# A graph network kernel: three node tiles fetched by TensorE in two turns of three, and the work between its two layers in another order

## What is computed

```python
h = jnp.maximum(_layernorm(x, axis=-1), 0.0)
x = x + layer_one(h, node_vec1, src, dst, edge_attr_4, edge_attr_64, ...)
h = jnp.maximum(_layernorm(x, axis=-1), 0.0)
# layer two, per edge and then per node:
ss, vv = (s[src], v[src])
out0 = C0 * (ss * e0 @ W1 + dot * INV3 @ W2)
out1 = C1 * (p3 + p4 + p5)          # products of ss, vv with e0, e1
m_agg = jax.ops.segment_sum(m, dst, num_segments=n)
x = x + jax.nn.relu(m_agg through Ws, Wv) + h
```

## Time and profile before

| | us |
|---|---|
| median of 3 runs | 1985.27 (1984.33 to 1985.97) |
| the profiled execution, its time | 1984.93 |
| its span, first to last instruction | 1983.0 |
| GpSimd busy | 1434.7 (72%) |
| TensorE busy | 1687.1 (85%) |
| VectorE busy | 1275.5 (64%) |
| ScalarE busy | 174.6 (9%) |

### The profile page before, as it was taken

One profiled execution on the slowest core, in us unless ns is written; L12 is line 12 of the kernel. 1 busy time (PEld: TensorE's weight loads), 2 busy tenths in 40 slices (PEclk: granted clock), 3 DMA queues, 4 the chain that ended last, 5 costly groups with the idle time before them and its releaser, 6 DMA issues.

```text
span 1983.0 us, 52527 instructions
## 1 busy us (share of the span) xinstructions
PE 1687.1 (85%) x15596; PEld 1447.7 (73%) x15596; DVE 1275.5 (64%) x2725; ACT 174.6 (9%) x392; POOL 1434.7 (72%) x1531
## 2 busy tenths in 40 slices
PE   6988999889898888998867878888787878788787
PEld 4766676767676666676647878787787878788787
DVE  6887888788877787787866444454544445454543
ACT  5100000000000010001050000000000000000000
POOL 2777777777777777777736777777777777777774
PEclk9999999999999998999978999898989989898988
DMA  6333333333333333333313232223232332332323
GB/s 234 104 101 102 102 103 101 103 102 102 102 103 101 103 102 102 102 103 101 102 41 87 70 75 72 73 72 73 72 74 70 74 74 70 74 74 70 74 71 83
DMA packets 112032, 179.50 MB, mean 91 GB/s; under 512 B 30382, under 2 KB 79212, under 8 KB 111628
## 3 DMA queue, kind: packets, MB, share of 16 engines
q0 software_dynamic: 71904, 122.81, 25.3%
q1 hardware_dynamic: 35208, 51.38, 8.2%
q10 hardware_dynamic: 4644, 2.19, 0.4%
HBM read 170.11 MB, written 6.14 MB: 89 GB/s over the span
## 4 chain that ended last, share of the span: by engine, by line
POOL 64%; issue 22%; PE 8%; DVE 2%; DMA 2%; ACT 1%; POOLq 1%; DVEq 0%; ACTq 0%
POOL g L663 64%; PE w_ps L953 2%; PE sums L942 2%; DMA g<-node_table,src 1%; PE sums L963 1%; PE sums L953 1%; PE w_ps L469 1%; DVE work L814 1%; PE w_ps L905 1%; PE sums L938 0%; ACT H L281 0%; POOLq L657 0%; DVE work L808 0%; PE hid_ps L891 0%; PE w_ps L1115 0%
## 5 line engine op out<-in xcount | busy, mean ns | idle before, releaser
L663 POOL DMA_INDIRECT g<-node_table,src x1498 | 1420.2, 948 | 487.0 <-issue 472.9
L942 PE MATMUL sums<-g,sel 128*128 128x160 f32 x1612 | 292.2, 343 | 158.4 <-DMA g<-node_table,src 157.3
L953 PE MATMUL w_ps<-H,work 128*128 128x160 f32 x2900 | 405.2, 300 | 2.6 <-DVE work L778 2.6
L953 PEld LDWEIGHTS w_ps<-H,work 128*128 128x128 f32 x2900 | 398.0, 191 | 2.9 <-DVE work L778 2.9
L942 PEld LDWEIGHTS sums<-g,sel 128*128 128x128 f32 x1612 | 269.7, 222 | 171.3 <-DMA g<-node_table,src 139.0
L814 DVE TENSOR_TENSOR work<-w_ps,g 128x384 f32<-128x384 f32 (+3 forms) x693 | 298.7, 459 | 107.1 <-DMA g<-node_table,src 56.6
L833 DVE STREAM_TRANSPOSE turned<-sums 128x160 f32<-128x160 f32 x232 | 80.0, 345 | 433.4 <-PE sums L963 296.7
L905 PE MATMUL w_ps<-fc_sb,work 64*128 64x224 f32 x1612 | 239.4, 397 | 88.4 <-DVE work L808 76.3
L938 PEld LDWEIGHTS sums<-work,sel 128*32 128x32 f32 x6448 | 201.6, 113 | 110.6 <-issue 72.9
L905 PEld LDWEIGHTS w_ps<-fc_sb,work 64*128 64x128 f32 x1612 | 174.0, 200 | 135.8 <-DVE work L808 106.4
L761 DVE TENSOR_TENSOR sel<-mixed,sh 128x896 f32<-128x896 f32 x232 | 251.7, 1085 | 27.7 <-DVE mixed L757 2.2
(11 more groups left out here) (81 smaller groups left out, 524.1 us busy)
## 6 DMA issues: line engine op xcount, KB each, us to landing
g<-node_table SPq DMA_DIRECT2D x2304, 0.6 KB
feat<-edge_feat_dram SPq DMA_DIRECT2D x60, 512.0 KB
g<-node_table,src POOLq DMA_INDIRECT x1498
g<-node_table ACTq DMA_DIRECT2D x1152, 0.6 KB
named<-src_rows_dram SPq DMA_DIRECT2D x30, 128.0 KB
X<-x_dram SPq DMA_DIRECT2D x5, 400.0 KB, 6.6
node_table<-H SPq DMA_DIRECT2D x5, 400.0 KB, 2.7
named<-src_rows_dram SPq DMA_DIRECT2D x30, 64.0 KB
```

The lines of the kernel that those rows point to most:

```text
L663: nc.gpsimd.indirect_dma_start(out=g[:, slot(p, u, j), :], out_offset=None, in_=table[layer], in_offset=bass.IndirectOffsetOnAxis(ap=src[: ...
L942: last = nc.tensor.matmul(sums[:, o % 2, 0:D], sel[:, o % 2, j, :], g[:, slot(p, o % UNROLL, j), :], **first_last)
L953: last = nc.tensor.matmul(found_at[:, i, 0:D], match[layer][:, i, t, :], H[:, t, :], start=(t == 0), stop=(t == NT - 1))
```

## The change

1. In layer two, in turns p = 0 and p = 1 of each period, TensorE fetches tile 6 of group 1 too (`MORE_AT`, `PICK_ROWS`): 18 fetches more and 18 gathers less. The third match has a buffer of its own, in `acc0`, which layer one no longer needs, and the numbers of the semaphores are computed anew (`pick_number`). Names for three picks instead of two are loaded every turn.
2. In the last turn of layer one (groups 112 to 115) the fetch for group 114 and its match are gone, and GpSimd gathers that tile.
3. Between the layers ScalarE computes all 25 gates first, then two square roots (parts of 18 and 7 tiles), then normalises tiles 0 to 10. VectorE normalises tiles 11 to 24, in two rounds of seven, as a scale and shift per tile and one maximum with zero over all seven. The table is written in four pieces (6, 5, 7 and 7 tiles), and VectorE adds `H` to `X` in two steps ahead of layer two's preparation.

```diff
-ROOTS = (0, 11, 21, NT)
+ROOTS = (0, 18, NT)
+BY_ACT = 11
+PIECES = (0, 6, BY_ACT, 18, NT)
...
+MORE_AT = ((), (0,1))
+PICK_ROWS = ((2,), (0, 1, 2))
...
-        acc0 = sb("acc0", [ROWS[0], 2, ACC_W])
+        acc0_all = sb("acc0", [P, 2, ACC_W])
+        acc0 = acc0_all[0:ROWS[0], :, :]
...
-        match = (acc1[:, 1:2, 0:NPAD].rearrange("p b (t e) -> p b t e", e=P),
-                 work[:, 0:2 * NPAD].rearrange("p (b t e) -> p b t e", b=2, e=P))
+        by_tile = lambda row: row.rearrange("p (t e) -> p t e", e=P)
+        match = ((by_tile(acc1[:, 1, 0:NPAD]),),
+                 (by_tile(work[:, 0:NPAD]), by_tile(work[:, NPAD:2 * NPAD]), by_tile(acc0_all[:, 0, 0:NPAD])))
...
-            picked = PICKED[layer]
-            picks = len(picked)
-            by_pool = [TILES - (u in picked) for u in range(UNROLL)]
-
-            def pick_after(o, s, ahead):
-
-
-                u = (o + ahead) % UNROLL
-                if not own_weights and u in picked and (s is None or s + ahead < GROUPS):
-                    return picked.index(u), (o + ahead) // UNROLL
+            more_at, pick_rows = MORE_AT[layer], PICK_ROWS[layer]
+
+            def picks_of(p):
+
+                return pick_rows if p in more_at else PICKED[layer]
+
+            def picks_before(f, p, e):
+
+                n = len(more_at)
+                return len(PICKED[layer]) * f + (n * e + (n if p < 0 else sum(m < p for m in more_at)) if n else 0)
+
+            def pick_number(f, p, e, i, nxt=0):
+
+                if nxt:
+                    f, p, e = f + 1, (p + 1 if p != PERIOD - 1 else 0), (e + 1 if p in (-1, PERIOD - 1) else e)
+                return picks_before(f, p, e) + i
+
+            def pick_after(o, s, p, ahead):
+
+                u, nxt = (o + ahead) % UNROLL, (o + ahead) // UNROLL
+                then = picks_of((p + 1) % PERIOD if nxt and p >= -1 else p)
+                if not own_weights and u in then and (s is None or s + ahead < GROUPS):
+                    return then.index(u), nxt
                 return None
+
+            def fetched(p, s, u):
+
+                return u in picks_of(p) and not (own_weights and s is not None and s >= GROUPS - UNROLL)
...
-                    tiles = min(tiles_of(UNROLL * it + u), by_pool[u] - by_row_at(p, u, TILES - 1))
+                    tiles = min(tiles_of(UNROLL * it + u), TILES - fetched(p, UNROLL * it + u, u) - by_row_at(p, u, TILES - 1))
...
-                        if o == 1 and (s is None or s < GROUPS):
-                            put(f, 0, 0, s == 1)
+                        if o == 1:
+                            if fetched(p, s, 2):
+                                put(f, p, e, 2, 0, 0, s == 1)
+                            else:
+                                act.sem_inc(found_copied, 1)
                     else:
                         if s == 0:
-                            put(f, 0, 0, True)
-                        if pick_after(o, s, 1):
-                            put(f, *pick_after(o, s, 1), s is not None and s + 1 < UNROLL)
+                            put(f, p, e, 0, 0, 0, True)
+                        if pick_after(o, s, p, 1):
+                            put(f, p, e, (o + 1) % UNROLL, *pick_after(o, s, p, 1), s is not None and s + 1 < UNROLL)
...
                     if not fresh:
-                        dve.wait_ge(found, picks * f + (picks * nxt + i + 1 - picks))
+                        dve.wait_ge(found, m if own_weights else m - 1)
                     wide = [P, NT, P]
-                    nc.vector.tensor_tensor(match[layer][:, i, :, :], wanted.unsqueeze(1).to_broadcast(wide),
+                    nc.vector.tensor_tensor(match[layer][i], wanted.unsqueeze(1).to_broadcast(wide),
...
-                                compare(f, 0, 1, False)
+                                if s == GROUPS - 1 - UNROLL:
+                                    dve.wait_ge(named_in[layer], 16 * f + 32)
+                                    dve.sem_inc(named_read, 1)
+                                    dve.sem_inc(match_done, 1)
+                                else:
+                                    compare(f, p, e, 2, 0, 1, False)
...
-                            find(f, 0, 0)
-                        if pick_after(o, s, 1):
-                            find(f, *pick_after(o, s, 1))
-                    elif o == 1 and (s is None or s < GROUPS):
-                        find(f, 0, 0, s == 1)
+                            find(f, p, e, 0, 0)
+                        if pick_after(o, s, p, 1):
+                            find(f, p, e, *pick_after(o, s, p, 1))
+                    elif o == 1:
+                        if fetched(p, s, 2):
+                            find(f, p, e, 0, 0, s == 1)
+                        else:
+                            pe.sem_inc(found, 1)
...
-            def finish(n):
-                act.wait_ge(norm1_ready, n + 1)
-                for u in parts[n]:
-                    normalise(u, h1_ready)
-
             nc.scalar.activation(warm[:], zero[:], ACT.Sigmoid)
             for t in range(NT):
                 gate(t)
-                if t == parts[0][-1] + 4:
-                    root(act, parts[0], 0, var1_step, root1_done)
-                    act.wait_ge(norm1_ready, 1)
-                u = t - (parts[0][-1] + 4)
-                if 0 <= u < len(parts[0]):
-                    normalise(u, h1_ready)
-            for u in range(max(0, NT - (parts[0][-1] + 4)), len(parts[0])):
+            root(act, parts[0], 0, var1_step, root1_done)
+            act.wait_ge(norm1_ready, 1)
+            root(act, parts[1], 1, var1_step, root1_done)
+            for u in range(BY_ACT):
                 normalise(u, h1_ready)
...
-                if t == parts[0][-1] + 4:
-                    invert(dve, parts[0], 0, root1_done, norm1_step, norm1_ready)
-            invert(dve, parts[1], 1, root1_done, norm1_step, norm1_ready)
-            invert(dve, parts[2], 2, root1_done, norm1_step, norm1_ready)
+            for n, tiles in enumerate(parts):
+                invert(dve, tiles, n, root1_done, norm1_step, norm1_ready)
+                dve.wait_ge(norm1_ready, n + 1)
+                own = range(max(tiles[0], BY_ACT), tiles[-1] + 1)
+                for u in own:
+                    last = nc.vector.tensor_scalar(H[:, u, :], X[:, u, :], rstd[:, u:u + 1], shift[:, u:u + 1], ALU.mult, ALU.add)
+                last.then_inc(scaled, 1)
+                dve.wait_ge(scaled, n + 1)
+                at = slice(own[0], own[-1] + 1)
+                nc.vector.tensor_scalar(H[:, at, :], H[:, at, :], 0.0, None, ALU.max).then_inc(h1_by_dve, 1)
+            dve.wait_ge(h1_by_dve, len(parts))
+            nc.vector.tensor_tensor(X[:, BY_ACT:, :], X[:, BY_ACT:, :], H[:, BY_ACT:, :], ALU.add).then_inc(added, 1)
+            dve.wait_ge(h1_ready, BY_ACT)
+            nc.vector.tensor_tensor(X[:, 0:BY_ACT, :], X[:, 0:BY_ACT, :], H[:, 0:BY_ACT, :], ALU.add).then_inc(added, 1)
             dve.wait_ge(acc1_clear, 2)
             then = Steps(dve, edge_set)
             windows(then)
             dve.wait_ge(pair_in, 64)
             nc.vector.tensor_tensor(pair[:], pair[:], pair_k[:], ALU.mult)
             nc.vector.tensor_tensor(wout[:], wout[:], wout_k[:], ALU.mult).then_inc(weights_ready, 1)
-            dve.wait_ge(h1_ready, NT)
-            nc.vector.tensor_tensor(X[:], X[:], H[:], ALU.add).then_inc(added, 1)
...
-            for tiles in parts:
+            for n, tiles in enumerate(pieces):
                 at = slice(tiles[0], tiles[-1] + 1)
-                sp.wait_ge(h1_ready, tiles[-1] + 1)
+                if tiles[0] < BY_ACT:
+                    sp.wait_ge(h1_ready, tiles[-1] + 1)
+                else:
+                    sp.wait_ge(h1_by_dve, n - len(pieces) + len(parts) + 1)
```

71 lines of the change are left out of this document (35 added, 36 removed).

## The result

| | before | after |
|---|---|---|
| median of the runs, us | 1985.62 (1984.33 to 1986.2, 4 runs) | 1963.85 (1963.11 to 1964.9, 4 runs) |
| profiled execution, its time | 1984.93 | 1964.47 |
| its span | 1983.0 | 1962.6 |
| granted clock, whole span | 0.920 | 0.946 |

The ratio is 0.9892, 95% interval 0.9876 to 0.9907: the change makes the kernel 21.8 us faster. The forecast was 1961.9, in a range of 1958.8 to 1969.0.

The account below looks back on a forecast made before the run. GpSimd's gathers were taken to bound the kernel. Gains of 22.5 + 0.2 + 1.1 = 23.8 us, less 0.4 for the tail, net 23.4, gave 1961.9 us, in a range of 1958.8 to 1969.0.

Parts of the forecast that it names:

- What bounds the kernel: Whole kernel: GpSimd's gathers, 64% of the span plus 22% on issue; layer two goes by their number while TensorE has room.
- Part 1: Layer two: 18 gathers fewer at 1.250 us each, 22.5 us gained; TensorE needs 86.2 us per period against GpSimd's 92.5.
- Part 2: Last turn of layer one, fetch removed: the last gather lands about 2.55 us after its start, 0.2 us gained.
- A sign of being wrong: Last turn of layer one: sums of 4 us in group 114 would point to Rival A.
- Rival A: Last turn of layer one and end of layer two: rests cost clock, 3.7 us in all, time 1965.2 us; chance 0.14.
- Part 3: Between the layers: arithmetic wins 4.5 us, bunched table writes leave 1.1 us; nothing with VectorE at its upper bound.
- The tail: End of layer two: 0.4 us given back, a quarter of the 1.7 us the linear step loses at half clock.

Follow-up runs that it names:

- The load held back: The changed kernel with SyncE's last feature load of layer one waiting for the last products: median 1968.37 us, ratio 0.9902; profiled execution 1959.83 us.
- Part 3 alone: The kernel before with only the new stretch between the layers, fetch kept: 3195.61 us on a slow chip, within 0.3% of the kernel before there.
- part 1 alone: The kernel before with only layer two's extra fetches (`MORE_AT`, `PICK_ROWS`, third match): 1969.63 us, ratio 0.9905.

## Why the prediction was right, and where it was off

**What bounds the kernel: right.** GpSimd's gathers, with the same share of the chain after as before.

**Part 1: right, in size and in mechanism.** 18 gathers less; the stretch shrinks by 23.44 us, of which 1.12 is the shorter first gather, so 22.3 against 22.5. TensorE's need per period was foreseen at 86.2 us and was 87.1; the rest of 5.29 us went, the clock from 1100 to 1900 us rose from 0.91 to 0.97, and no gather waits for a sum longer than the ordinary 0.30 us. ScalarE was the closest call: for the copy of group 1 a margin of 1.3 us was foreseen and 0.1 us was there, and the copy for the next group 0, which was not worked out, came 2.2 us behind its fetch. The second half of the argument carried, since TensorE needs that copy only 6.5 us later still.

**Part 2: the step that failed.** The term was -0.2 and is +3.95. "It will start at 998.20, and lands about 2.55 us after its start, as an earlier one did": the start was right, the landing 5.03. The prediction took the duration of a transfer from a row in which no load of features was near (the engines moved 61 to 93 GB/s from 971 to 975 us, gathers among them), passed over the gather that lands in 4.07 us beside such a load in the same trace, and didn't ask what the removed fetch had been holding back. The list of what waits for TensorE's next instruction behind the fetch would have shown it: `hid` of the last group, and behind that SyncE's load. The load held back puts the landing at 2.56 us and the term at -0.56. A sign of being wrong that the prediction had named, a sum of some 4 us in group 114, did come.

**Rival A** was half of it. The sum at half clock is there (3.94 for 2.11 us), priced at 2.0 and worth 1.8, but it stands behind the late gather and not behind the removed fetch by itself: with the load held back the fetch is as absent, TensorE rests 1.44 us and the sum runs at full clock. The Trainium skill's rule ("TensorE: Matmul & The Clock Gate", Part 1: the throttled state is the default, activity releases it) names the cost that came. The trace agrees, with a granted clock of 0.50 behind 5.51 us of rest; the rest itself came from the late landing. The time lies between forecast and A, 1.95 us above the one and 1.35 below the other. That it lies so near the forecast is in part luck: the other half of the loss, the late landing, stands in no rival, and gains elsewhere hide some of it.

**Part 3: the order of events right, two sizes off.** Counted from the first gate product, which came 3.95 us late, ScalarE's 11 tiles were foreseen to end at 1042.35 and ended at 1042.22. VectorE's two rounds were taken at half of their upper bound, 4.25 us, and took 1043.30 - 1037.40 = 5.9: seven steps take 2.00 us and the maximum 0.74, so a round is 2.8 us where 4.0 was the bound and 2.0 was taken. So VectorE and not ScalarE ends last, by 1.1 us, and the last seven tiles are written then; since the writes are bunched anyway, 0.9 us stay of the 1.1 foreseen. The first gather was left at 3.50 us because no row says why it is long, with 2.5 us as the bound; it became 2.38, and 1.19 with the pieces in another order, though the second gather then takes 1.34 instead of 0.95. Part 3 alone shortens it and part 1 alone does not, and the order of the writes by itself changes it; which piece of part 3 does the rest, and why, stays open.

**The tail: right in that nothing came.** 0.4 us was given back and 0.0 was due; the linear step ran at half clock before and after (4.08 us in both). So there was nothing for it to lose, neither the 0.4 nor the 1.7 us that rival A had for it.

**In sum**, of the span's 3.0 us, part 2 is 4.15 worse and the gathers 0.2, against 0.9 better between the layers (first gather included) and 0.4 in the tail. In the medians it is 1.95 us, because the profiled execution of the changed kernel is 0.6 us above its median, and that of the kernel before was 0.3 to 0.7 below.

## What to carry to other kernels

Before you take an operation away, list what stands behind it on its engine and what that releases on the queues: an instruction that is no longer delayed may start a transfer just when the critical one is under way. Price a transfer that becomes the last to arrive by what else will move beside it, not by its usual landing. A load that runs ahead "for the next turn" has no use in the last one, and here it lay beside the transfer that the end of the layer waited for: skip it there or hang it on something late, and look at whole times as well, which here did not confirm the gain.

## What the runs showed of the hardware

- An indirect gather of one tile beside a load of 512 KB issued 0.04 us earlier landed in 5.03 us, and in 2.56 us with the load out of its way; in the first case the DMA engines moved 343 GB/s from 1000 to 1001 us. In the kernel before a gather landed in 4.07 us with such a load issued 2.3 us ahead of it.
- A linear step after a rest of 2.71 us ran at 2.41 us in one kernel and at 4.08 us in another with the same order, so the rest just before doesn't decide the level by itself; after 5.51 us of rest the granted clock was 0.50 and 56 records of a sum took 3.94 us instead of 2.11.
- The first gather after a table has been written took 3.50 us in the kernel before and 2.38 in the changed one. On one chip it took 2.39 and, with nothing but the order of the writes changed, 1.19, the next one then 1.34 instead of 0.95.
- Gathers took 946 ns in some executions and 949 in others of much the same code, 4.4 us over the kernel; and two chips ran this program in 3200 us, with rests of 1.8 to 2.5 us between single matmuls in the rows shown, while code that runs once took its usual time. Why isn't shown by these runs.
